# A four-layer network on one core: order of TensorE's work in the state space layers, and quantised stages rebuilt with features on partitions

## The chip, the cores and the metric
The kernel runs on one core of a Trainium2 chip. The metric is the device time of one execution in microseconds, median of the runs. All arithmetic is in float32.

## The reference, cut to what matters
The input x is 8 sequences of 256 tokens with 128 features. Twelve sublayers follow each other; the change touches the second of the middle group (state space layers) and the two quantised feed-forward networks near the end.
```python
for i in range(4):                       # state space layers; x is the normalised input
    xn = layernorm(x, ln_w[i], ln_b[i])
    x_in, z = split(xn @ in_w.T); xc = silu(conv4(x_in) + cb)
    dt_rank, Bm, Cm = split(xc @ xp_w.T); dt = softplus(dt_rank @ dt_w.T + dt_b)
    h_t = h_{t-1} * exp(dt_t * A) + dt_t * xc_t * B_t        # 256 channels x 16 states
    y = sum_n(h_t * C_t) + xc * D
    x = (y * silu(z)) @ out_w.T + x
...
h = x                                     # quantised network; x is the normalised input
for b in range(3):
    y = h @ (dequant(q[2b]) + lb @ la).T + bias[2b]
    y = gelu(layernorm(y, gamma[b], beta[b]))
    h = y @ (dequant(q[2b+1]) + lb @ la).T + bias[2b+1] + h
# used as: x = x + 0.5 * h, before and after the last attention
```

## The kernel before, in words
Each sublayer is a stage of its own with a barrier behind it, at which its semaphores are cleared. x stays on the chip, tokens on partitions. Within a stage every engine has its own instruction stream, in an order written out by hand, and semaphores tie them together. An engine never passes an instruction that waits.

**State space layers** (`state_space_layers`). A unit (l, s) is layer l of sequence s; 32 units follow each other in `over_units`. A unit has NP = 8 slots, one for each pair of states. In slot i: ScalarE makes the decays of slot i + 1 in two PSUM banks (`decays`, L1301, four Exp of 255 columns), VectorE multiplies dt·u by the B rows (`input_term`, L1151; GpSimd does slot 4) and scans (L1173), GpSimd multiplies the state by the C rows one slot later (L1225), TensorE adds these up with the identity as stationary operand two slots later (L1382, four passes a slot) into `y_bank`. In slot 0 of that lag the skip product comes behind it (L1387), in slot 2 the gated result (`yg`, L1158) of the last unit goes through the output product (L1396) together with the old x (L1393), and ScalarE copies it back into `xm` (L1324, slot 4).

The pieces of the next unit (`nxt`) and the one after it (`after`) are prepared in the same slots by `prepare`: slot 0 the xp product, 1 its rows (ScalarE, L1256), 2 the dt product (TensorE, L1349) and Abs and Exp of it (ScalarE, L1259, L1261), 3 two Identities and Ln (L1264 to L1267, Ln and the next Exp each need a table load), 4 the normalised rows of `after` (ScalarE, L1276), 5 their transposes and the gate product of `nxt` (TensorE), 6 the convolution product (L1368), 7 Silu of both (L1286, L1292). On TensorE `prepare(i)` comes last in slot i, behind the sum, the skip product and the output product. All preparation goes through PSUM bank 7.

`stage_state_space` writes the normalised input to `xm`; after the layers a block of its own adds `xm` to x (L1038).

**Quantised stages** (`stage_quantised_ffn`, tags f3a and f3b). Both make the weights `w` anew from the packed integers. The 8 sequences go in two rounds of U = 4. For each of 3 blocks the four sequences pass through one phase after the other: transpose h (L2010), copy, product y with tokens on partitions (L2018), bias added and statistics by VectorE (L1933, L1910, L1913), rstd by GpSimd (L1962, L1965), normalised (L1918), transposed (L2026), Gelu (L1990), second product (L2034), added to h plus bias (L1945, GpSimd L1973).

Of the kernel before, what the change touches and what calls it, by code (L numbers as in the profile page):

```python
# [11 lines left out]
ALU = mybir.AluOpType  # L12
# [3 lines left out]
P = 128  # L16
# [18 lines left out]
    "f3": dict(scale=768, bias=768, la=768, lb=768, gam=3, bet=3),  # L35
# [912 lines left out]
def stage_state_space(K, tag):  # L948
# [3 lines left out]
    with ExitStack() as scope:  # L952
# [92 lines left out]
def state_space_layers(K, tag, m):  # L1045
# [12 lines left out]
    with ExitStack() as scope:  # L1058
# [44 lines left out]
        with nc.Block() as block:  # L1103
# [143 lines left out]
            def _(act):  # L1247
                def prepare(i, nxt, after):
# [62 lines left out]
                def slot(i, now, last, nxt, after):  # L1311
# [23 lines left out]
            def _(pe):  # L1335
# [37 lines left out]
                def slot(i, now, last, nxt, after):  # L1373
                    at = lagged(i, 2, NP, now, last)
# [24 lines left out]
                    prepare(i, nxt, after)  # L1399
# [468 lines left out]
def stage_quantised_ffn(K, tag):  # L1868
    nc = K.nc
    NB, U = 3, 4  # L1870
    with ExitStack() as scope:
        K.scope = scope
        sb = K.sb
        w = sb(f"{tag}_w", [P, 6 * P])
        bn = sb(f"{tag}_bn", [P, U, TS, 6])
        mv = sb(f"{tag}_mv", [P, U, TS, 2])
        rs = sb(f"{tag}_rs", [P, U, TS])
        hcur = sb(f"{tag}_h", [P, U, W])
        hb = sb(f"{tag}_h_bias", [P, U, W])
        ht = sb(f"{tag}_ht", [P, U, W])  # L1880
        y = sb(f"{tag}_y", [P, U, W])
        yn = sb(f"{tag}_yn", [P, U, W])
        gt = sb(f"{tag}_gelu_t", [P, U, W])
        (dve_s, pool_s, lora_ps, w_ready, stats, rstd, h_ready, ht_ps, ht_ready, y_ps, yn_ready, ynt_ps, gt_ready,
         z_ps, hb_ready, pool_hold, y_sb) = make_sems(
            K, tag, "dve_chain pool_chain lora_product w_ready stats rstd h_ready ht_product ht_ready y_product "
                    "yn_ready ynt_product gelu_ready z_product h_bias_ready pool_hold y_ready")
        f = lambda n: field(K, "f3", n)
        bias = f("bias")
        NL = (NB + 1) * U  # L1890
        with nc.Block() as block:
# [3 lines left out]
            def _(dve):  # L1895
                dve.wait_ge(K.loaded["f3"], 16)
                dve.wait_ge(K.loaded_q, 16)
                link = chain(dve, dve_s)

                link(dve.tensor_scalar(w[:, :], K.qw[:, :], 7.5, 1.0 / 7.5, ALU.subtract, ALU.mult))  # L1900
                link(dve.tensor_tensor(w[:, :], w[:, :], f("scale"), ALU.mult))
                dve.wait_ge(lora_ps, 1)
                dve.tensor_tensor(w[:, 0:512], w[:, 0:512], K.ps[0][:, :], ALU.add).then_inc(w_ready, 1)
                dve.tensor_tensor(w[:, 512:768], w[:, 512:768], K.ps[1][:, 0:256], ALU.add).then_inc(w_ready, 1)
                with dve.Fori(0, B // U) as s:
                    link = chain(dve, dve_s)

                    def statistics(u, src):
                        for j in range(TS):
                            i = dve.bn_stats(bn[:, u, j, :], src(j))  # L1910
                        link(i)
                        for j in range(TS):
                            i = dve.bn_aggr(mv[:, u, j, :], bn[:, u, j, :])  # L1913
                        i.then_inc(stats, 1)

                    def normalise(u, src, dst):
                        for j in range(TS):
                            i = dve.tensor_scalar(dst[:, u, j * P:(j + 1) * P], src(j), mv[:, u, j, 0:1],  # L1918
                                                  rs[:, u, j:j + 1], ALU.subtract, ALU.mult)
                        return i  # L1920

                    xt = lambda u: lambda j: K.x[:, bass.ds((s * U + u) * W + j * P, P)]
                    yt = lambda u: lambda j: y[:, u, j * P:(j + 1) * P]
                    for u in range(U):
                        statistics(u, xt(u))
                    for u in range(U):
                        dve.wait_ge(rstd, s * NL + u + 1)
                        normalise(u, xt(u), hcur).then_inc(h_ready, 1)
# [669 lines left out]
```

## Time and profile before

| | |
|---|---|
| median of 3 runs | 3105.43 us (3095.72 to 3110.03) |
| the profiled execution | 3106.51 us |
| its span, first to last instruction | 3104.8 us |
| mean granted TensorE clock | 0.896 of full speed |
| busy: PE, DVE, ACT, POOL | 83%, 65%, 55%, 40% of the span |

"Idle before" is the time in which the engine waited for the instruction named as releaser. Records of matmuls overlap, since the last columns of one drain while the next streams.

### The profile page before, as it was taken

How to read it: one execution, taken by the hardware profiler on the slowest of the kernel's cores; microseconds unless marked ns; L12 is line 12 of the kernel's file. 1: busy time of each engine (PE TensorE's matmuls, PEld its weight loads, DVE VectorE, ACT ScalarE, POOL GpSimd, SP SyncE). 2: the span in 40 equal slices, each digit the busy share in tenths (PEclk: the TensorE clock that was granted, in tenths of full speed). 3: DMA queues.
4: the chain of work that ended last, by engine and by line, in shares of the span. 5: the costliest groups of instructions: out<-in, count | busy, mean ns of one | idle time of the engine just before them, and what ended most of it. 6: DMA issues, size and time to landing. Idle time of an engine off the chain costs nothing. (4 is left out here: it accounts for less than half of the span.)

```text
span 3104.8 us, 39498 instructions
## 1 busy us (share of the span) xinstructions
PE 2575.9 (83%) x11320; PEld 1549.7 (50%) x11320; DVE 2025.0 (65%) x4275; ACT 1696.5 (55%) x3585; POOL 1243.8 (40%) x1144
## 2 busy tenths in 40 slices
PE   7999785688888888888677998688699967988975
PEld 5667532354444444444333443456444444777764
DVE  7888655699999999999644443466344364545445
ACT  4555322788888888888422443577444323555532
POOL 1000102688888888888500000322000052444444
PEclk9999898798989989989898999799899966888866
DMA  2000131333333434333332111000111100000000
GB/s 99 1 1 0 58 83 28 131 142 136 151 140 139 145 136 150 140 136 148 143 82 82 55 60 50 1 1 0 55 55 55 63 15 0 1 0 0 0 1 14
DMA packets 35669, 209.60 MB, mean 68 GB/s; under 512 B 4032, under 2 KB 5184, under 8 KB 14016
## 3 DMA queue, kind: packets, MB, share of 16 engines
q1 hardware_dynamic: 35520, 207.89, 18.8%
q8 instruction: 60, 0.98, 0.1%
q14 instruction: 89, 0.73, 0.1%
HBM read 205.25 MB, written 2.62 MB: 67 GB/s over the span
## 5 line engine op out<-in xcount | busy, mean ns | idle before, releaser
L1382 PE MATMUL banks<-mam_state_c,identity 128*128 128x512 f32 x1024 | 539.7, 662 | 141.8 <-POOL mam_state_c L1225 141.8
L1225 POOL TENSOR_TENSOR mam_state_c<-mam_state,weights_r 128x1024 f32<-128x1024 f32 x256 | 599.9, 2358 | 118.6 <-DVE mam_state L1173 118.5
L1173 DVE TENSOR_TENSOR_SCAN mam_state<-banks,mam_dbu 128x1024 f32<-128x1024 f32 x256 | 580.4, 2278 | 73.1 <-ACT banks L1301 72.5
L1301 ACT ACTIVATE banks<-mam_dt,mam_a_neg 128x255 f32<-128x255 f32 x1024 | 423.3, 461 | 38.3 <-DVE mam_state L1173 36.7
L1382 PEld LDWEIGHTS banks<-mam_state_c,identity 128*128 128x128 f32 x1024 | 200.1, 208 | 399.1 <-issue 199.6
L1151 DVE TENSOR_TENSOR mam_dbu<-banks,weights_r 128x1024 f32<-128x1024 f32 x224 | 267.1, 1204 | 10.4 <-ACT banks L1309 10.4
L2224 POOL TENSOR_TENSOR at_attention<-at_relu 128x512 f32<-128x512 f32 x128 | 130.9, 1040 | 172.9 <-ACT at_relu L2277 88.3
L424 ACT ACTIVATE at_probs<-banks,at_nmax 128x256 f32<-128x256 f32 x256 | 117.7, 472 | 138.4 <-DVE at_nmax L365 134.9
L2402 PEld LDWEIGHTS banks<-at_v,at_attention 128*128 128x128 f32 x1024 | 153.2, 223 | 41.0 <-issue 34.8
L862 DVE TENSOR_TENSOR m2b_hidden<-m2b_gelu,m2b_comb_spread 128x512 f32<-128x512 f32 x128 | 85.9, 690 | 129.2 <-ACT m2b_gelu L889 119.6
L862 DVE TENSOR_TENSOR m2a_hidden<-m2a_gelu,m2a_comb_spread 128x512 f32<-128x512 f32 x128 | 86.0, 690 | 128.9 <-ACT m2a_gelu L889 118.5
L2402 PE MATMUL banks<-at_v,at_attention 128*128 128x64 f32 x1024 | 152.6, 303 | 4.2 <-POOL at_attention L2224 4.2
L889 ACT ACTIVATE m2b_gelu<-banks,weights_r 128x512 f32<-128x512 f32 x128 | 85.2, 685 | 105.2 <-PE banks L909 105.2
L889 ACT ACTIVATE m2a_gelu<-banks,weights_r 128x512 f32<-128x512 f32 x128 | 85.2, 685 | 105.0 <-PE banks L909 104.9
L930 PE MATMUL banks<-m2a_hidden,weights_r 128*128 128x512 f32 x256 | 123.0, 604 | 7.1 <-DVE m2a_hidden L862 7.1
L930 PE MATMUL banks<-m2b_hidden,weights_r 128*128 128x512 f32 x256 | 123.0, 604 | 6.6 <-DVE m2b_hidden L862 6.6
L1706 ACT ACTIVATE at_probs<-at_scores,at_negated_max 128x160 f32<-128x160 f32 x256 | 95.0, 421 | 59.1 <-DVE at_negated_max L1553 58.8
L909 PE MATMUL banks<-m2b_xnt,weights_r 128*128 128x512 f32 x256 | 123.5, 606 | 0.0
L144 POOL TENSOR_SCALAR at_ln_rs<-at_ln_mv 128x2 f32<-128x2 f32 x16 | 4.5, 282 | 294.3 <-DVE at_ln_mv L346 252.9
L909 PE MATMUL banks<-m2a_xnt,weights_r 128*128 128x512 f32 x256 | 122.3, 600 | 0.0
L1368 PE MATMUL banks<-mam_xn_padded,weights_r 128*128 128x256 f32 x512 | 120.8, 390 | 0.7 <-ACT mam_xn_padded L1281 0.7
L1368 PEld LDWEIGHTS banks<-mam_xn_padded,weights_r 128*128 128x128 f32 x512 | 100.4, 196 | 29.0 <-issue 14.3
(483 smaller groups left out, 5304.6 us busy)
## 6 DMA issues: line engine op xcount, KB each, us to landing
weights_r<-mam_bc_rows SPq DMA_DIRECT2D x128, 1024.0 KB, 4.7
m2a_comb_spread<-m2a_comb_rows SPq DMA_DIRECT2D x16, 1024.0 KB, 7.6
m2b_comb_spread<-m2b_comb_rows SPq DMA_DIRECT2D x16, 1024.0 KB, 7.6
m1a_comb_spread<-m1a_comb_rows SPq DMA_DIRECT2D x16, 512.0 KB, 8.1
m1b_comb_spread<-m1b_comb_rows SPq DMA_DIRECT2D x16, 512.0 KB, 8.5
weights_r<-in_mb SPq DMA_DIRECT2D x1, 4332.0 KB, 12.8
weights_r<-in_m SPq DMA_DIRECT2D x1, 4200.0 KB, 13.1
weights_r<-in_a SPq DMA_DIRECT2D x1, 2632.0 KB, 12.1
```

Source lines behind the costliest of these rows:

```text
L862: dve.tensor_tensor(hid[:, g % 3, c, :], gelu[:, g % 2, c, :], comb[:, block_of(p, e // 4) + e % 4, :], ALU.mult).then_inc(hid_ready, 1)
L889: act.activation(gelu[:, g % 2, c, :], h_bank(g, c)[:, :], ACT.Gelu, bias=b1[:, 2 * e + c:2 * e + c + 1]).then_inc(gelu_ready, 1)
L909: pe.matmul(h_bank(g, c)[:, :], w1[:, e * 256 + c * P:e * 256 + (c + 1) * P], R.xnt[:, p % 2, :], start=True, stop=True).then_inc(h_ps, 1)
L930: i = pe.matmul(y[:, :], w2[:, (2 * e + c) * P:(2 * e + c + 1) * P], hid[:, g % 3, c, :], start=False, stop=(e == E - 1 and c == 1))
L1151: dve.tensor_tensor(dbu[:, j % 4, :, :, :], both(K.ps[6][:, :].rearrange("p (c t) -> p c t", c=C)), b_rows(j), ALU.mult).then_inc(dbu_dve, 1)
L1173: dve.tensor_tensor_scan(flat2(h[:, i % 4, :, :, :]), decay(i), flat2(dbu[:, i % 4, :, :, :]), 0.0, ALU.mult, ALU.add).then_inc(h_ready, 1)
L1225: pool.tensor_tensor(hc[:, j % 4, :, :, :], h[:, j % 4, :, :, :], c_rows(j), ALU.mult).then_inc(hc_ready, 1)
L1301: i = act.activation(decay(j)[:, o + 1:o + S], dt[:, q, c, 1:S], ACT.Exp, scale=aneg[:, l, k:k + 1])
L1368: k = pe.matmul(K.ps[7][:, c * S:(c + 1) * S], f(l, "taps")[:, t * 256 + c * P:t * 256 + (c + 1) * P], xpad[:, q, t:t + S], start=(t == 0) ...
L1382: k = pe.matmul(y_bank(q)[:, :], K.ident[:, :], flat(hc[:, j % 4, n, :, :]), start=(j == 0 and n == 0), stop=(j == NP - 1 and n == 1))
L2224: pool.tensor_tensor(at[:, i % 4, :, :], rel[:, i % 4, :, :], rel[:, i % 4, :, :], ALU.mult).then_inc(at_ready, 1)
L2402: k = pe.matmul(K.ps[4 + g % 2][:, t * 256 + r * DV:t * 256 + (r + 1) * DV], at[:, h % 4, j, t * P:(t + 1) * P], v[:, q, j, h * DV:(h + 1) ...
```

## The change
In the state space layers TensorE calls `prepare(i)` first in slot i instead of last. ScalarE issues its two Identities in slot 2, right behind Exp and ahead of the decays that it makes in slot 3 (those of slot 4); Ln stays in slot 3. In the last layer TensorE adds x to the output product with the identity, and ScalarE writes the result to x; the closing addition and its block are gone.

The quantised stages are written anew. Features are on partitions throughout, and the work goes in N = 12 steps m: block m // 4, pair of sequences m % 4 (512 tokens). In slot m TensorE issues the second product z of step m - 4, the spread of rstd over the partitions for step m - 2, the sum of squares over the partitions for step m - 1 and the first product y of step m. The mean over features is taken out of the weights and the bias beforehand, so that only the variance is left to compute: Square on ScalarE, products with a column of ones, a small operation on VectorE, the power on GpSimd, a product of the broadcast column with the identity. The weights are made once, in f3a, and kept. The input is normalised and transposed pair by pair at the start; at the end each pair is transposed back and added to x. The bias comes as six columns in place of 768.
```diff
-    "f3": dict(scale=768, bias=768, la=768, lb=768, gam=3, bet=3),
+    "f3": dict(scale=768, bcol=6, la=768, lb=768, gam=3, bet=3),
...
         state_space_layers(K, tag, dict(locals()))
-        clear_sems(K)
-        add_s, = make_sems(K, tag, "added")
-        with nc.Block() as block:
-            @block.vector
-            def _(dve):
-                dve.tensor_tensor(K.x[:, :], K.x[:, :], xm[:, :], ALU.add).then_inc(add_s, 1)
-                dve.wait_ge(add_s, 1)
 
...
-                    if nxt and i == 3:
                         act.wait_ge(exp_ready, b + 1)
                         act.activation(vu[:, :, :], ve[:, :, :], ACT.Identity, bias=K.ones[:, 0:1]).then_inc(plus_ready, 1)
                         act.wait_ge(plus_ready, b + 1)
                         act.activation(va[:, :, :], vu[:, :, :], ACT.Identity, bias=K.neg_one[:, 0:1]).then_inc(part_ready, 1)
+                    if nxt and i == 3:
                         act.activation(vl[:, :, :], vu[:, :, :], ACT.Ln).then_inc(ln_ready, 1)
                     if after:
                         l, s, q = after
...
-                        act.activation(xm[:, bass.ds(s * W, W)], y_bank(q)[:, 0:W], ACT.Copy).then_inc(done, 1)
+                        res = K.x if l + 1 == L else xm
+                        act.activation(res[:, bass.ds(s * W, W)], y_bank(q)[:, 0:W], ACT.Copy).then_inc(done, 1)
...
                 def slot(i, now, last, nxt, after):
+                    prepare(i, nxt, after)
                     at = lagged(i, 2, NP, now, last)
...
                                       xm[:, bass.ds(s * W + t * P, P)], start=True, stop=False)
+                            if l + 1 == L:
+                                pe.matmul(y_bank(q)[:, t * P:(t + 1) * P], K.ident[:, :],
+                                          K.x[:, bass.ds(s * W + t * P, P)], start=False, stop=False)
                             for c in range(C):
                                 k = pe.matmul(y_bank(q)[:, t * P:(t + 1) * P], yg[:, c, t * P:(t + 1) * P],
                                               f(l, "outw")[:, c * P:(c + 1) * P], start=False, stop=(c == C - 1))
                         k.then_inc(out_ps, 1)
-                    prepare(i, nxt, after)
 
...
+                    firsts = w[:, :].rearrange("p (b a o) -> p b a o", b=NB, a=2)[:, :, 0, :]
+                    link(dve.tensor_reduce(wmean[:, :], firsts, AX_X, ALU.add))
+                    link(dve.tensor_scalar(wmean[:, :], wmean[:, :], 1.0 / P, None, ALU.mult))
+                    dve.tensor_tensor(firsts, firsts, wmean[:, :].unsqueeze(2).broadcast_to([P, NB, P]), ALU.subtract)
...
+                for m in range(N + 5):
+                    n = m - 4
+                    if 0 <= n < N:
+                        dve.wait_ge(z_ps, n + 1)
+                        h = ht[:, n % NP, :]
+                        dve.scalar_tensor_tensor(h, z_bank(n)[:, :], b2(n), h, ALU.add, ALU.add).then_inc(h_ready, 1)
+                    n = m - 2
+                    if 0 <= n < N:
+                        dve.wait_ge(r_ps, n + 1)
+                        dve.wait_ge(y_ready, n + 1)
+                        if n >= 2:
+                            dve.wait_ge(gt_ready, n - 1)
+                        dve.tensor_tensor(yn[:, n % 2, :], yc[:, n % 3, :], r_bank(n)[:, :],
+                                          ALU.mult).then_inc(yn_ready, 1)
+                    n = m - 1
+                    if 0 <= n < N:
+                        dve.wait_ge(var_ps, n + 1)
+                        if n >= 2:
+                            dve.wait_ge(ys_ready, n - 1)
+                        dve.tensor_scalar(var[:, n % 2, :], v_cols(n), 1.0 / P, EPS, ALU.mult,
+                                          ALU.add).then_inc(var_ready, 1)
+                    if m + 2 < NP:
+                        norm_sums(m + 2)
+                        norm_apply_pair(m + 2)
+                    p = m - 5 - (NB - 1) * NP
+                    if 0 <= p < NP:
+                        dve.wait_ge(o_ps, p + 1)
+                        x = K.x[:, p * WP:(p + 1) * WP]
+                        dve.scalar_tensor_tensor(x, y_bank(m)[:, :], 0.5, x, ALU.mult, ALU.add).then_inc(added, 1)
 
...
+                for n in range(N):
+                    if n + 2 < NP:
+                        norm_root(n + 2)
+                    pool.wait_ge(var_ready, n + 1)
+                    if n >= 2:
+                        pool.wait_ge(r_ps, n - 1)
+                    pool.tensor_tensor(ys[:, n % 2, :], var[:, n % 2, :], K.neg_half[:, 0:TP],
+                                       ALU.pow).then_inc(ys_ready, 1)
...
+                for m in range(N + 2):
+                    n = m - 2
+                    if 0 <= n < N:
+                        act.wait_ge(yn_ready, n + 1)
+                        if n >= 2:
+                            act.wait_ge(z_ps, n - 1)
+                        act.activation(gt[:, n % 2, :], yn[:, n % 2, :], ACT.Gelu, bias=f("bet")[:, n // NP:n // NP + 1],
+                                       scale=f("gam")[:, n // NP:n // NP + 1]).then_inc(gt_ready, 1)
+                    if m < N:
+                        act.wait_ge(y_ps, m + 1)
+                        if m >= 2:
+                            act.wait_ge(var_ps, m - 1)
+                        act.activation(sq[:, m % 2, :], y_bank(m)[:, :], ACT.Square, bias=b1(m)).then_inc(sq_ready, 1)
+                        if m >= 3:
+                            act.wait_ge(yn_ready, m - 2)
+                        act.activation(yc[:, m % 3, :], y_bank(m)[:, :], ACT.Identity, bias=b1(m)).then_inc(y_ready, 1)
+                    if m + 1 < NP:
+                        transposed_input(m + 1)
 
             @block.tensor
...
+                for m in range(N + 5):
+                    n = m - 4
+                    if 0 <= n < N:
+                        pe.wait_ge(gt_ready, n + 1)
+                        if n < 2:
+                            pe.wait_ge(ht_ready, n + 3)
+                        else:
+                            pe.wait_ge(h_ready, n - 1)
+                        c = 2 * (n // NP) + 1
+                        pe.matmul(z_bank(n)[:, :], w[:, c * P:(c + 1) * P], gt[:, n % 2, :],
+                                  start=True, stop=True).then_inc(z_ps, 1)
+                    n = m - 2
+                    if 0 <= n < N:
+                        pe.wait_ge(ys_ready, n + 1)
+                        if n < 2:
+                            pe.wait_ge(ht_ready, n + 1)
+                        else:
+                            pe.wait_ge(yn_ready, n - 1)
+                        for j in range(TP):
+                            k = pe.matmul(r_bank(n)[:, j * P:(j + 1) * P], ys[:, n % 2, j:j + 1].broadcast_to([P, P]),
+                                          K.ident[:, :], start=True, stop=True)
+                        k.then_inc(r_ps, 1)
+                    n = m - 1
+                    if 0 <= n < N:
+                        pe.wait_ge(sq_ready, n + 1)
+                        if n >= 1:
+                            pe.wait_ge(var_ready, n)
+                        for j in range(TP):
+                            k = pe.matmul(v_cols(n)[:, j:j + 1], sq[:, n % 2, j * P:(j + 1) * P], K.ones[:, 0:1],
+                                          start=True, stop=True)
+                        k.then_inc(var_ps, 1)
+                    if m < N:
+                        p = m % NP
+                        if m >= 3:
+                            pe.wait_ge(y_ready, m - 2)
+                        if m < NP:
+                            pe.wait_ge(ht_ready, m + 1)
+                        else:
+                            pe.wait_ge(h_ready, m - NP + 1)
+                        c = 2 * (m // NP)
+                        pe.matmul(y_bank(m)[:, :], w[:, c * P:(c + 1) * P], ht[:, p, :],
+                                  start=True, stop=True).then_inc(y_ps, 1)
+                        if m + 1 < NP:
+                            transposed_input(m + 1)
+                    p = m - 5 - (NB - 1) * NP
+                    if 0 <= p < NP:
+                        pe.wait_ge(h_ready, (NB - 1) * NP + p + 1)
+                        pe.wait_ge(y_ready, min(N, m - 2))
+                        if p >= 3:
+                            pe.wait_ge(added, p - 2)
+                        for j in range(TP):
+                            k = pe.transpose(y_bank(m)[:, j * P:(j + 1) * P], ht[:, p, j * P:(j + 1) * P], K.ident[:, :])
+                        k.then_inc(o_ps, 1)
...
```

## Rows read from the trace of the kernel before

**Rows 1.** The page, busy times and the granted clock in 40 slices of 77.6 us.
```profile
...
PE 2575.9 (83%) x11320; PEld 1549.7 (50%) x11320; DVE 2025.0 (65%) x4275; ACT 1696.5 (55%) x3585; POOL 1243.8 (40%) x1144
...
PEclk9999898798989989989898999799899966888866
...
```

**Rows 2.** Windows by stage: length, busy PE, PEld, DVE, ACT, POOL, clock, DMA.
```profile
...
1200.00:1400.00 200.00, 171.33 (x516) 93.17 (x515) 182.51 (x142) 166.15 (x334) 174.35 (x109) 0.91 0.39 142
2480.00:2584.00 104.00, 63.72 (x300) 51.32 (x300) 63.89 (x252) 21.38 (x48) 50.88 (x112) 0.70 0.05 18
...
```

**Rows 3.** Waits of DVE, ACT, PE in 620 to 1460 us: total, times, longest.
```profile
...
DVE mam_state L1173 <- ACT banks L1301: 65.2, 43, 1.9
...
ACT mam_dt_abs L1259 <- PE banks L1349: 80.8, 28, 3.0
...
ACT mam_conv L1286 <- PE banks L1368: 18.2, 14, 1.4
...
PE banks L1382 <- POOL mam_state_c L1225: 114.5, 59, 3.5
...
```

**Rows 4.** Groups of instructions, 620 to 1460 us: busy, mean ns, idle before.
```profile
...
L1173 DVE TENSOR_TENSOR_SCAN mam_state<-banks,mam_dbu 128x1024 f32<-128x1024 f32 x226 | 512.6, 2278 | 65.4 <-ACT banks L1301 65.2
...
L1301 ACT ACT_TABLE_LOAD x56 | 71.8, 1283 | 1.0
...
L1142 DVE SCALAR_TENSOR_TENSOR mam_dt_correction<-banks,mam_dt_correction 128x512 f32<-128x512 f32 x28 | 19.2, 686 | 2.4 <-POOL mam_dt_correction L1189 0.2
...
```

**Rows 5.** Timeline of parts of two units: start, duration, instruction, idle before.
```profile
...
1006.76 3.78 PE L1382 MATMUL banks<-mam_state_c,identity 128*128 128x512 f32 x4 [3.31 <-POOL mam_state_c L1225]
...
1012.47 2.12 PE L1382 MATMUL banks<-mam_state_c,identity 128*128 128x512 f32 x4
...
1022.39 3.70 PE L1382 MATMUL banks<-mam_state_c,identity 128*128 128x512 f32 x8
...
1028.22 1.13 PE L1349 MATMUL banks<-mam_bc_dt_rows,weights_r 9*128 9x256 f32 x4
...
1029.39 0.60 ACT L1259 ACTIVATE mam_dt_abs<-banks 128x512 f32<-128x512 f32 x1 [2.88 <-PE banks L1349]
...
1038.66 2.29 DVE L1173 TENSOR_TENSOR_SCAN mam_state<-banks,mam_dbu 128x1024 f32<-128x1024 f32 x1 [1.86 <-ACT banks L1301]
1038.73 0.87 ACT L1276 ACTIVATE mam_ln_xn<-mam_xm,mam_ln_bias,mam_ln_rs 128x128 f32<-128x128 f32 x2
...
```

**Rows 6.** Timeline at the end of the state space layers.
```profile
...
1526.82 0.38 ACT L1324 ACTIVATE mam_xm<-banks 128x256 f32<-128x256 f32 x1 [10.89 <-PE banks L1396]
1530.20 2.29 DVE L1038 TENSOR_TENSOR x<-x,mam_xm 128x2048 f32<-128x2048 f32 x1 [5.08 <-PEq L67]
...
1533.36 0.87 DVE L604 BATCH_NORM_STATS2 m1b_ln_bn<-x 128x6 f32<-128x128 f32 x4 [0.86 <-PEq L67]
...
```

**Rows 7.** Timeline, first and last work of both quantised stages.
```profile
...
2480.64 2.87 PE L1998 MATMUL banks<-weights_r 32*128 32x128 f32 x12 [2.92 <-PEq L67]
...
2580.85 1.35 DVE L1950 SCALAR_TENSOR_TENSOR x<-f3a_h,x 128x256 f32 x3
...
2997.36 2.90 PE L1998 MATMUL banks<-weights_r 32*128 32x128 f32 x12 [4.00 <-PEq L67]
...
3096.01 1.79 DVE L1950 SCALAR_TENSOR_TENSOR x<-f3b_h,x 128x256 f32 x4
...
```

**Rows 8.** Durations of like operations, from timelines and a group.
```profile
...
1535.06 1.02 POOL L547 TENSOR_TENSOR m1b_ln_rs<-m1b_ln_rs,neg_half 128x4 f32<-128x4 f32 x1
...
1538.50 0.60 ACT L652 ACTIVATE m1b_xnt<-banks 128x512 f32<-128x512 f32 x1 [11.30 <-PE banks L556]
...
1539.15 1.89 PE L563 MATMUL banks<-weights_r,m1b_xnt 128*128 128x16 f32 x8 [0.69 <-ACT m1b_xnt L652]
...
L889 ACT ACTIVATE m2a_gelu<-banks,weights_r 128x512 f32<-128x512 f32 x128 | 85.2, 685 | 105.0 <-PE banks L909 104.9
...
2505.50 1.06 PE L2018 MATMUL banks<-f3a_w,f3a_ht 128*128 128x128 f32 x8
...
```

More of the change, by code:

```diff
@@ L1888, in stage_quantised_ffn @@
-        f = lambda n: field(K, "f3", n)
-        bias = f("bias")
-        NL = (NB + 1) * U
+        w = K.f3_w
+        wmean = sb(f"{tag}_w_mean", [P, NB])
+        bcol = K.f3_b
+        bn = sb(f"{tag}_bn", [P, NP, TP, 6])
+        mv = sb(f"{tag}_mv", [P, NP, TP, 2])
+        rs = sb(f"{tag}_rs", [P, NP, TP])
+        xn = sb(f"{tag}_xn", [P, 2, WP])
+        ht = sb(f"{tag}_ht", [P, NP, WP])
+        yc = sb(f"{tag}_y", [P, 3, WP])
+        sq = sb(f"{tag}_y_squares", [P, 2, WP])
+        var = sb(f"{tag}_y_var", [P, 2, TP])
@@ L1891, in stage_quantised_ffn @@
+        f = lambda n: field(K, "f3", n)
+        first = tag == "f3a"
+        y_bank = lambda m: K.ps[m % 3]
+        r_bank = lambda m: K.ps[3 + m % 2]
+        z_bank = lambda m: K.ps[5 + m % 2]
+        t_bank = lambda p: (r_bank, z_bank)[p // 2](p)
+        b1 = lambda m: bcol[:, 2 * (m // NP):2 * (m // NP) + 1]
+        b2 = lambda m: bcol[:, 2 * (m // NP) + 1:2 * (m // NP) + 2]
+        v_cols = lambda m: K.ps[7][:, (m % 2) * 8:(m % 2) * 8 + TP]
         with nc.Block() as block:
@@ new lines, in norm_root @@
+                def norm_root(p):
+                    pool.wait_ge(stats, p + 1)
+                    pool.tensor_scalar(rs[:, p, :], mv[:, p, :, 1], EPS, None, ALU.add).then_inc(eps_in, 1)
+                    pool.wait_ge(eps_in, p + 1)
+                    pool.tensor_tensor(rs[:, p, :], rs[:, p, :], K.neg_half[:, 0:TP], ALU.pow).then_inc(rstd, 1)
+                norm_root(0)
+                norm_root(1)
+                for n in range(N):
[6 more added lines that the diff above has]
+                                       ALU.pow).then_inc(ys_ready, 1)
@@ L1979, in _, with transposed_input @@
             @block.scalar
             def _(act):
-                act.wait_ge(K.loaded["f3"], 16)
-                with act.Fori(0, B // U) as s:
-                    for b in range(NB):
-                        e = s * (NB * U) + b * U
-                        for u in range(U):
-                            act.wait_ge(ht_ps, e + u + 1)
-                            act.activation(ht[:, u, :], K.ps[0 + u % 2][:, 0:W], ACT.Copy).then_inc(ht_ready, 1)
-                        for u in range(U):
-                            act.wait_ge(ynt_ps, e + u + 1)
-                            act.activation(gt[:, u, :], K.ps[4 + u % 2][:, 0:W], ACT.Gelu, bias=f("bet")[:, b:b + 1],
-                                           scale=f("gam")[:, b:b + 1]).then_inc(gt_ready, 1)
+                def transposed_input(p):
+                    act.wait_ge(xt_ps, p + 1)
+                    act.activation(ht[:, p, :], t_bank(p)[:, :], ACT.Copy).then_inc(ht_ready, 1)
@@ new lines, in _, with transposed_input @@
+                if first:
+                    for i in range(6):
+                        k = pe.matmul(K.ps[i // 4][:, (i % 4) * P:(i % 4 + 1) * P], f("la")[0:32, i * P:(i + 1) * P],
+                                      f("lb")[0:32, i * P:(i + 1) * P], start=True, stop=True)
+                    k.then_inc(lora_ps, 1)
+                    pe.matmul(K.ps[2][:, 0:6], K.ones[:, :], f("bcol"), start=True, stop=True).then_inc(bias_ps, 1)
+                def transposed_input(p):
+                    pe.wait_ge(xn_ready, p + 1)
+                    for j in range(TP):
+                        k = pe.transpose(t_bank(p)[:, j * P:(j + 1) * P], xn[:, p % 2, j * P:(j + 1) * P], K.ident[:, :])
+                    k.then_inc(xt_ps, 1)
@@ L2566, in host_arrays @@
     g["f3"] = dict(scale=np.repeat(i["L3_ffn_scales"].transpose(2, 0, 1), 16, axis=0).reshape(P, -1),
-                   bias=rows(i["L3_ffn_biases"]), la=pad(i["L3_ffn_lora_a"].transpose(1, 0, 2).reshape(32, -1)),
+                   bcol=i["L3_ffn_biases"].T, la=pad(i["L3_ffn_lora_a"].transpose(1, 0, 2).reshape(32, -1)),
                    lb=pad(i["L3_ffn_lora_b"].transpose(2, 0, 1).reshape(32, -1)),
```

182 lines of the change are left out of this document (54 added, 128 removed).

## The prediction, blind

> **What bounds the kernel now.** I read the page first: PE is busy 83% of the span, DVE 65%, and the granted clock is lowest, 0.6 to 0.8 of full, in slices 33 and 34 and in the last two [rows 1]. Those are the two quantised stages. The windows by stage then say what kind of stage each is. In the state space layers DVE is busy 182.5 of 200 us, POOL 174, PE 171, ACT 166: four nearly full engines. In a quantised stage nothing is full: PE and DVE 64 of 104 us, ACT 21, at a clock of 0.70 [rows 2]. The first is short of one engine's time, the second is a chain in which engines take turns.
>
> State space layers. A unit is one sequence of one layer, 32 in all, of 8 slots. The 226 scans in 840 us are 28.25 units, so a unit takes 29.7 us. DVE waits 65.2 us there, all for ACT's decays: 2.3 us a unit, so DVE's own floor is 29.7 - 2.3 = 27.4 us. ACT in turn waits 80.8 us, 28 times, in front of Abs for the dt product of PE (2.9 us a unit), and 18.2 us for the convolution product. PE waits for POOL 114.5 us, 4.05 a unit [rows 3, 4]. The timeline shows why the dt product is late. PE works without a break from the sum at 1006.76: through the sums of slots 5, 6, 7, 0 and 1 with the preparation between them, at 1022.39 the last sum of one unit and the first of the next (eight passes), then the skip product and the output product, and only at 1028.22 the dt product. ACT had stood 2.88 us when it got it, at 1029.39. Ln, two table loads and decays 5 follow on ACT, and the scan of slot 5 starts 1.86 us late, at 1038.66 [rows 5]. The reader should see that the order on PE, not its load, makes this wait: the sum, skip and output product in front are wanted by nobody yet.
>
> Quantised stages: from 2480.64 to 2582.2 (101.6 us) and from 2997.36 to 3097.8 (100.4 us) [rows 7].
>
> **Part 1, preparation ahead of the sums.** Nothing is removed, only order changes: dt is now issued before the slot's sum, skip and output product. From the last sum's end (1022.39 + 1.85 = 1024.2) to the dt product was 4.0 us and becomes nothing. ACT's two Identities (0.7 us each) move ahead of decays 4, where ACT has about 4 us in hand while scan 3 runs: no cost. No DMA is moved. What is queued behind the new position: in slot 5 the sum stands behind the transposes, which wait for ACT's normalised rows; in slots 0 and 6 sums stand behind the xp and convolution products. In return the convolution product comes one sum (1.7 us) earlier, which covers ACT's 18.2 us.
>
> What is late next? There are two loops. DVE's is its own work, 27.4 us. The other goes through PE: dt product, ACT to the end of its normalised rows (from 1028.22 to 1039.6 = 11.4 us, in which ACT does not idle after Abs), then PE from there to the last sum. That PE work is the same set as before, 1006.76 to 1024.2 = 17.4 us. Sum: 28.8 us, more than 27.4. But 17.4 contains a stretch at half clock: the four passes at 1006.76 take 3.78 us where eight take 3.70 at 1022.39, after an idle of 3.31 us [rows 5]. The half clock lasts until about the passes at 1012.47, which take 2.12 us for four again: 5.7 us, which cost half of that, 2.9 us, more than at full clock. Without it the loop is 25.9 us and DVE rules. The new idle ahead of slot 5, from sum 2's end to the normalised rows, I work out as 2.5 to 3.1 us, too near to 3.31 to say. So a unit is 27.4 to 28.8 us. I take the middle, 28.1: 1.6 us a unit, x 32 = 51 us. Bounds: 74 us (2.3 x 32) above; below, 28.8 us and 0.3 us more at each of the two places where sums now queue, 10 us. I keep 0 as a rival.
>
> **Part 2, last layer in place.** PE gets two products of 128 columns a unit in 8 units (0.4 us each, in PE's slack). DVE's addition goes with its block: after the last ACT instruction (1527.2) the long clearing stays, the addition (2.29 us) and the 0.86 us behind it go [rows 6]. Gain 3 us, bounds 2 and 5.
>
> **Part 3, quantised stages.** Work is now in steps of one pair of sequences and one block: 12 steps a stage, features on partitions, so that both transposes within a block vanish. For each step:
> PE: two products of 512 columns, each two passes. Eight such passes take 3.70 us with the last one's drain, a pitch of about 0.43 [rows 5], so 0.86 a product and 1.72 for two. The spread of rstd is four products of 128 columns, eight passes, 1.06 us by L2018 alone, 0.86 when others follow and its drain is covered [rows 8]. The variance is four products with one moving column but full 128-column loads: the nearest row is L563, eight passes of 16 columns in 1.89 us at half clock, so about 0.9 at full. Sum 3.5 us.
> ACT: Gelu, Square, Identity of 512 columns, 0.685 each by L889 [rows 8], 2.1 us. DVE: two operations of 512 columns at 0.69 by L1142 [rows 4] and a small one, 1.5 us. POOL: a power on 4 columns, 1.02 us [rows 8].
> PE is the longest. Does it run without gaps? In a slot of the new order z, the rstd spread and the variance are issued before y, and cover Square (y to variance of the next slot) and DVE's h (0.7 us, under 1.8 us of PE work). Variance, DVE, power (0.15 + 1.02) lies under y and z of 1.7 us. So in the middle PE sets the pace, at 3.5 us, and a busy PE keeps its clock; I take 3.6.
>
> The variance is where a page and a row part. The Trainium skill, "TensorE: Matmul & The Clock Gate", section "Wait — 56ns, not 53.3ns?", says that starts never come closer than about 25 ns however few the columns; by that alone, an estimate, the eight passes would take 0.2 us, a step 2.8 us and both stages 17 us less. No run here shows it; L563, which loads 128 columns per pass as this does, stands against it.
>
> Start of a stage: norm of a pair from 1533.36 to the end of the copy at 1539.1 is 5.7 us in a stage of the same form [rows 6, 8]. Then the first four steps can't fill PE: they wait for norms of pairs 2 to 4, which DVE does between them (a pair is 3.9 us from first statistic to normalised rows, two of which stand in front of the first variance), and at half clock. About 4 us a step: 16 us. Eight steps at 3.6: 29. Tail of the last pair: Square, variance, power, spread, multiply, Gelu, product, add, transpose, add: 0.7+0.9+0.2+1.0+0.9+0.7+0.7+0.9+0.7+0.5+0.7 = 7.9, with handovers 8. Together 5.7 + 16 + 29 + 8 = 58.7 us; 58 for f3b. f3a also makes its weights (conversion, scaling, two adds, mean and its removal, bias), partly beside the norm: 3 us more, 61. f3b loses that wholly. Gain 101.6 - 61 + 100.4 - 58 = 83 us. Bounds from both sides: a stage without start-up loss is 5.7 + 42 + 8 = 56, minus the variance's whole 0.9 x 12 that is 45 (gain 109 with f3a's 3 us); one with 5 us in all steps is 74 (gain 51).
>
> **Sum.** Profiled execution 3106.5 us (span 3104.8), 1.1 us above the median of 3105.4. 51 + 3 + 83 = 137. 3105.4 - 137 = 2968, I say 2969.
>
> **Rivals.** All in us of the median; likeliest case above, 0.50, own range 2945 to 2995.
> Clock kept, DVE rules the unit (27.4) and a quantised step is nearer 3.2: 74 + 3 + 93, 2935. For it: the new gap may stay under 3.31 us. Against: a gap of nearly that size stands in the same place. 0.18.
> The state space wait only changes its name: DVE's gating waits for the last sum, now behind one more product, and a unit stays 29.7. Gain 86, 3019. For it: PE is unbroken from 1006.76 to the dt product. Against: the reordered pieces are not on the loop. 0.12.
> Quantised steps bound by handovers or by table loads around Square (two of 1.28 us a step [rows 4] make ACT 4.6 us against 3.5): 1.1 x 12 x 2 = 26 less, 2995; at 5 us in the eight middle steps, 22 less and the first four longer too, 3000. Nothing in the trace shows a load ahead of a Square, and none shows Gelu with Square. 0.15.
> Slower: the half-clock stretch grows. In a unit it is now 5.7 us and costs 2.9. A unit must exceed 29.7 + 86/32 = 32.4 to undo parts 2 and 3; the loop is 25.9 + half the stretch, so the stretch must exceed 13 us. Then every further 2 us cost 32: at 18 us a unit is 34.9, 3186. The Trainium skill has this in "TensorE: Matmul & The Clock Gate", section "HAM oscillation": a PE that idles each round starts each round at half clock. Here the clock in the stage is 0.91, so it recovers each time. 0.03.
> The same clock in the quantised stages alone (steps of 7 us) takes the 83 away: 3051, still faster. 0.02.
>
> **Range and chances.** The first four cases cover 2935 to 3019, so 2930 to 3020 leaves out less than 0.2. A measurement of this kernel can't tell 0.5% (15 us) from nothing. All cases but the slower one are beyond it: faster 0.96, same 0.01, slower 0.03.
>
> **What the profile should show.** ACT's wait before Abs gone or under 0.5 us a unit; DVE's wait for decays under 1 us, perhaps a new DVE wait for the last sum before the gating; unit 28.1 us. Quantised stages of about 61 and 58 us, PE over 85% busy in their middle with the clock near full, variance passes near 0.11 us each, one table load at most. The prediction fails if the unit keeps its length, or if steps take over 4.5 us.

## The result and the profile after

The changed kernel takes 2966.8 us (2959.5 to 2970.5, 4 runs) against 3105.4 us; the ratio is 0.9555 (0.9525 to 0.9584). Forecast was 2969. The profiled execution has a span of 2963.2 us, 141.6 less than before.

The page first, against [rows 1]: slices 33 and 34, at a granted clock of 0.6 before, are at 0.8 now.
```profile
...
PE 2525.2 (85%) x11310; PEld 1514.2 (51%) x11310; DVE 1957.2 (66%) x3955; ACT 1711.4 (58%) x3566; POOL 1177.3 (40%) x960
...
PEclk9999989699999999999989999799989988899868
...
```
Windows of the same two kinds of stage, against [rows 2] (columns as there). The state space layers have DVE at 196 of 200 us instead of 182.5 (over the whole of 620 to 1400 us it is 757 of 780, at a clock of 0.94). The middle of a quantised stage has PE busy without a break, at full clock.
```profile
...
1200.00:1400.00 200.00, 175.43 (x579) 97.24 (x578) 195.95 (x152) 180.72 (x356) 185.52 (x118) 0.97 0.40 151
2446.00:2474.00 28.00, 28.00 (x162) 20.31 (x161) 12.76 (x25) 16.59 (x25) 8.05 (x8) 1.00 0.01 1
...
```
Waits in the state space layers, 620 to 1400 us, against [rows 3]: total, times, longest.
```profile
...
DVE mam_y_gated L1151 <- PE banks L1377: 17.7, 21, 1.4
DVE mam_state L1166 <- ACT banks L1294: 3.4, 8, 0.6
...
ACT mam_dt_abs L1252 <- PE banks L1343: 4.4, 6, 0.8
...
PE banks L152 <- ACT mam_ln_xn L1269: 84.5, 27, 3.3
...
```
In these 780 us there are 222 scans, 27.75 units. ACT's wait before Abs fell from 2.9 to 0.16 us a unit, DVE's wait for decays from 2.3 to 0.1. A new wait has come, the one the prediction named: DVE's gating waits 0.64 us a unit for the last sum. PE now idles 3.0 us a unit before the transposes. The timeline, against [rows 5]:
```profile
...
996.75 1.13 PE L1343 MATMUL banks<-mam_bc_dt_rows,weights_r 9*128 9x256 f32 x4
...
1007.70 0.86 ACT L1269 ACTIVATE mam_ln_xn<-mam_xm,mam_ln_bias,mam_ln_rs 128x128 f32<-128x128 f32 x2
...
1008.71 0.66 PE L152 MATMUL banks<-identity,mam_ln_xn 128*128 128x128 f32 x2 [3.26 <-ACT mam_ln_xn L1269]
...
1009.16 1.92 PE L1354 MATMUL banks<-mam_xn_padded,weights_r 128*128 128x256 f32 x4
...
1021.06 3.70 PE L1377 MATMUL banks<-mam_state_c,identity 128*128 128x512 f32 x8
...
1024.69 1.13 PE L1343 MATMUL banks<-mam_bc_dt_rows,weights_r 9*128 9x256 f32 x4
1024.80 0.69 DVE L1151 TENSOR_TENSOR mam_y_gated<-banks,mam_gate 128x512 f32<-128x512 f32 x1 [0.62 <-PE banks L1377]
...
1025.86 0.60 ACT L1252 ACTIVATE mam_dt_abs<-banks 128x512 f32<-128x512 f32 x1
...
```
The transposes come after an idle of 3.26 us, and the gate product behind them runs at half clock (1.92 us for four passes of 256 columns, 1.03 at full clock). The last sum of the unit (second half of the row at 1021.06; it ends at 1024.76, and the gating starts at 1024.80) is followed at once by the dt product, 1.2 us before Abs.

From the first scan to the end of the last there are 950.8 us before and 895.8 after: a unit is 29.71 and 27.99 us. This measure is used for all runs below. It comes from one profiled execution of each kernel; e7, which leaves the layers of the changed kernel as they are, gave 28.12, so differences of 0.1 us say nothing.

End of the layers, against [rows 6]: 3.0 us from the last ACT instruction to the next stage, where 6.2 us stood.
```profile
...
1471.78 0.38 ACT L1318 ACTIVATE x<-banks 128x256 f32<-128x256 f32 x1 [11.33 <-PE banks L1394]
...
1475.16 0.87 DVE L604 BATCH_NORM_STATS2 m1b_ln_bn<-x 128x6 f32<-128x128 f32 x4 [5.53 <-PEq L67]
...
```
Both quantised stages, against [rows 7]: f3a from 2419.40 to 2482.8, 63.4 us; f3b from 2897.30 to 2957.0, 59.7 us.
```profile
...
2419.40 0.87 DVE L1912 BATCH_NORM_STATS2 f3a_bn<-x 128x6 f32<-128x128 f32 x4 [2.05 <-PEq L67]
...
2426.75 2.07 PE L2089 MATMUL banks<-f3a_ht,f_weights 128*128 128x512 f32 x2 [1.33 <-DVE f_bias L1947]
...
2444.57 1.02 PE L2058 MATMUL banks<-f3a_gelu_t,f_weights 128*128 128x512 f32 x2
...
2462.09 1.02 PE L2058 MATMUL banks<-f3a_gelu_t,f_weights 128*128 128x512 f32 x2
...
2462.95 1.05 PE L2068 MATMUL banks<-identity,f3a_y_rs 128*128 128x128 f32 x8
...
2463.84 0.95 PE L2077 MATMUL banks<-ones,f3a_y_squares 128*128 128x1 f32 x8
...
2464.65 1.10 PE L2089 MATMUL banks<-f3a_ht,f_weights 128*128 128x512 f32 x2
...
2465.59 1.02 PE L2058 MATMUL banks<-f3a_gelu_t,f_weights 128*128 128x512 f32 x2
...
2482.09 0.69 DVE L1981 SCALAR_TENSOR_TENSOR x<-banks,x 128x512 f32<-128x512 f32 x1
...
```
```profile
...
2897.30 0.87 DVE L1912 BATCH_NORM_STATS2 f3b_bn<-x 128x6 f32<-128x128 f32 x4 [3.44 <-PEq L67]
...
2903.09 2.07 PE L2089 MATMUL banks<-f3b_ht,f_weights 128*128 128x512 f32 x2 [0.69 <-ACT f3b_ht L2006]
...
2917.70 1.92 PE L2058 MATMUL banks<-f3b_gelu_t,f_weights 128*128 128x512 f32 x2
...
2956.32 0.69 DVE L1981 SCALAR_TENSOR_TENSOR x<-banks,x 128x512 f32<-128x512 f32 x1 [0.15 <-PE banks L2100]
...
```
The five rows from 2462.09 are one step: z, spread, variance, y, and the next z 3.50 us later. Their starts are 0.81 to 0.94 us apart, with no idle noted.

### The profile page after: what moved, and what is told of

Its sections match the earlier page's. It is cut to its first block and busy times, and to the rows that moved or that the text cites. A ratio compares the mean times of both kernels' runs of the same rounds, so it can differ in the third digit from the quotient of the medians.

```text
span 2963.2 us, 38455 instructions
## 1 busy us (share of the span) xinstructions
PE 2525.2 (85%) x11310; PEld 1514.2 (51%) x11310; DVE 1957.2 (66%) x3955; ACT 1711.4 (58%) x3566; POOL 1177.3 (40%) x960
## 3 DMA queue, kind: packets, MB, share of 16 engines
q8 instruction: 62, 1.02, 0.1%
## 5 line engine op out<-in xcount | busy, mean ns | idle before, releaser
L1377 PE MATMUL banks<-mam_state_c,identity 128*128 128x512 f32 x1024 | 507.0, 633 | 9.9 <-POOL mam_state_c L1218 9.4
L152 PE MATMUL banks<-identity,mam_ln_xn 128*128 128x128 f32 x64 | 17.4, 363 | 127.6 <-ACT mam_ln_xn L1269 127.6
```

Of the source, the lines that this page charges most:

```text
L1377: k = pe.matmul(y_bank(q)[:, :], K.ident[:, :], flat(hc[:, j % 4, n, :, :]), start=(j == 0 and n == 0), stop=(j == NP - 1 and n == 1))
```

## The experiments

Every kernel is the one before or the changed one with one edit. A total also moves with stages that no edit touches: the last attention stage took 412.5 us in the changed kernel's profile, 402.9 in e4's and 398.6 in e12's, at granted clocks of 0.82, 0.84 and 0.86. So a unit's length is the better witness for the state space layers.

| run | unit, us | total, us | ratio to before |
|---|---|---|---|
| before | 29.71 | 3102 to 3105 | 1 |
| e1, TensorE's order alone | 30.26 | 3124.2 | 1.0063 (1.0041 to 1.0085) |
| e9, ScalarE's Identities alone | 29.52 | 3099.5 | 0.9981 (0.9967 to 0.9994) |
| e3, both | 28.24 | 3054.2 | 0.9845 (0.9818 to 0.9872) |
| e2, dt product alone | 28.72 | 3070.4 | 0.9897 (0.9874 to 0.992) |
| e11, before, gap filled | 29.16 | 3087.0 | 0.994 (0.9923 to 0.9957) |
| changed | 27.99 | 2966.8 | 0.9555 (0.9525 to 0.9584) |
| e4, changed, TensorE's order undone | 29.61 | 3004.2 | 0.9679 (0.9642 to 0.9717) |
| e5, changed, gap filled | 27.47 | 2939.7 | 0.9483 (0.9463 to 0.9504) |
| e10, two fillers | 27.56 | 2946.4 | 0.9493 (0.9477 to 0.9509) |
| e6, rows early | 28.79 | 2987.7 | 0.964 (0.9621 to 0.966) |
| e8, more work on TensorE | 28.72 | 2983.0 | 0.9613 (0.9587 to 0.9639) |
| e7, one variance product | 28.12 | 2955.9 | 0.9527 (0.9504 to 0.955) |
| e12, starts filled | 27.49 | 2946.9 | 0.9499 (0.9484 to 0.9515) |

**e1, TensorE's order alone.**
```diff
 def slot(i, now, last, nxt, after):       # TensorE
+    prepare(i, nxt, after)
     at = lagged(i, 2, NP, now, last)
...
-    prepare(i, nxt, after)
```

> The kernel before, with one edit: TensorE prepares first in each slot of the state space layers; ScalarE's order stays. My theory (the dt product came late because of the order on TensorE): the wait before Abs falls from 2.9 us a unit to under 0.5, a unit takes 28.1 to 28.3 us instead of 29.7, the total 3105 - 50 = 3055 us. Rival (the wait only changes its name, or ScalarE's move is what gives the gain): a unit stays above 29.2 us, the total 3090 or more.

It is 0.6% slower than before, and my theory fell as I had put it. The waits (620 to 1400 us, 25.5 units):
```profile
...
DVE mam_state L1173 <- ACT banks L1301: 42.5, 36, 1.7
DVE mam_y_gated L1158 <- PE banks L1383: 35.9, 26, 1.4
...
ACT banks L1301 <- DVE mam_state L1173: 65.3, 75, 1.7
...
```
The timeline shows the chain. ACT makes Abs and Exp early, then waits 1.74 us for a scan before decays 4, and only behind them come the Identities, the normalised rows, and PE's transposes after an idle of 4.68 us:
```profile
...
1000.35 1.12 PE L1349 MATMUL banks<-mam_bc_dt_rows,weights_r 9*128 9x256 f32 x4
...
1004.51 1.66 ACT L1301 ACTIVATE banks<-mam_dt,mam_a_neg 128x255 f32<-128x255 f32 x4 [1.74 <-DVE mam_state L1173]
...
1006.12 0.71 ACT L1264 ACTIVATE mam_dt_one_plus<-mam_dt_exp,ones 128x512 f32<-128x512 f32 x1
...
1012.71 0.87 ACT L1276 ACTIVATE mam_ln_xn<-mam_xm,mam_ln_bias,mam_ln_rs 128x128 f32<-128x128 f32 x2
...
1013.72 0.66 PE L152 MATMUL banks<-identity,mam_ln_xn 128*128 128x128 f32 x2 [4.68 <-ACT mam_ln_xn L1276]
...
```
From the dt product to the end of the rows it is 13.2 us, not 11.4. PE's work from the transposes to the end of the last sum takes 17.4 us as before, and the next dt product starts 30.7 us after this one. So DVE waits for the last sum (1.4 us a unit) and still for decays (1.7).

**e2, only the dt product first.** Edit: `if i == 2: prepare(...)` ahead of the sum, all other slots behind it.

> The kernel before, with only the preparation of slot 2 (the dt product) ahead of its sum, all other slots as before. If the dt product carries the gain: a unit of 28.3 us, the total about 3062 us; the wait of 0.65 us a unit before the convolution's Silu stays. Rival (the convolution product, the transposes and xp being earlier carry it): 29.2 us a unit or more, 3090.

A unit of 28.72 us, between the 28.3 of the theory and the 29.2 of the rival: this one move gives 1.0 us, with the Identities unmoved. The sum of slot 5 isn't held up by the transposes here. What stays is what the later pieces would bring:
```profile
...
DVE mam_state L1173 <- ACT banks L1301: 25.1, 31, 1.4
...
ACT mam_xn_padded L1281 <- PE banks L152: 32.3, 23, 2.2
ACT mam_conv L1286 <- PE banks L1368: 22.7, 22, 1.6
...
```
**e3, order and Identities, and e9, Identities alone.**
```diff
-                    if nxt and i == 3:
                         act.wait_ge(exp_ready, b + 1)
                         act.activation(vu[:, :, :], ve[:, :, :], ACT.Identity, ...)
                         act.wait_ge(plus_ready, b + 1)
                         act.activation(va[:, :, :], vu[:, :, :], ACT.Identity, ...)
+                    if nxt and i == 3:
                         act.activation(vl[:, :, :], vu[:, :, :], ACT.Ln)
```

> The kernel before with the whole of part 1, TensorE's order and ScalarE's two Identities. Theory: the Identities are hidden, so this is within 5 us of the run with TensorE's order alone, near 3053 us. Rival: the Identities cost, or give, 10 us or more.

> The kernel before with ScalarE's two Identities in slot 2 alone. TensorE's order alone was slower than before (3124 us), both were 3054, and undoing TensorE's order in the changed kernel gave 3004 where 3024 was forecast. Theory now: the Identities fill the time in which ScalarE would wait for a scan, so moving them is worth about 20 us with the old order of TensorE and 70 with the new: 3083 us here, a unit of 29.1 us. Rival (the 20 us came with the quantised stages or the last layer in place): 3103 us.

The total of e3 is the one expected, but the reason was wrong: it is 2.0 us a unit shorter than e1, not equal. e9 is 0.2 us a unit shorter than before. So the Identities are worth 0.2 us with the old order and 2.0 with the new. With the new order ACT has Exp done while a scan runs; put there, the Identities fill the wait. With the old order Abs came so late (74.0 us of waiting in 780 in e9) that there was no such wait to fill. The forecast for e9, 3083 us and a unit of 29.1, was missed: the 20 us that it sought to explain in e4 are not the Identities'.

**e4, TensorE's order undone in the changed kernel.** The reverse of e1's edit.

> The changed kernel with TensorE preparing last again. Theory: parts add up, so the unit returns to 29.7 us and the total is 3105 - 79 (quantised stages by the trace after) - 3 = 3023 us. Rival (the parts overlap, or the last layer in place already helped the state space layers): under 3010 us.

3004 us, 19 less than expected. The unit is 29.61, as forecast. The two profiled executions say where the rest lies. e4's is 98.1 us shorter than that of the kernel before: 3 from the first scan to the last, 3 at the end of the last layer, 82 in the quantised stages (61.6 and 58.0 us here) and 10 in the untouched attention stage between them (405.0 us from the end of f3a to the start of f3b, against 415.2). So the parts add up in the layers, and the rival's overlap is not what made the total short; why the attention stage was shorter stays open.

**e5, the gap filled, and e10, filled less.** Five (e10: two) products with a zero stationary operand, added behind slot 4's sum; the result doesn't change.
```diff
+                        if j == 2:
+                            for n in range(5):
+                                pe.matmul(y_bank(q)[:, 0:S], zero[:, :], skip[:, 0, :, :].rearrange("p c t -> p (c t)"),
+                                          start=False, stop=False)
```

> The changed kernel; in slot 4 TensorE adds, behind the sum, five products of a zero stationary operand with 256 constant columns (ten passes, 2.1 us), so that it idles 1.2 us instead of 3.3 before the transposes. Result unchanged. Theory (the half-clock stretch behind that gap is what keeps a unit at 28.1 us above VectorE's 27.4): the granted clock in the layers goes from 0.94 to near 1.00, VectorE's wait for the last sum goes, a unit takes 27.5 us, the total 2967 - 19 = 2948 us. Rival (order and handovers set it, not the clock): 2967 us or more, for TensorE has more to do.

> The changed kernel with two zero products of 256 columns (0.85 us) behind slot 4's sum instead of five. Theory (the clock falls because of the idle, and a shorter idle of about 2.4 us keeps most of it): granted clock 0.98 or more in the layers, 2945 us. Rival (only an idle near 1 us keeps it, as five products left): clock near 0.94, 2960 us or more.

Waits and window of e5:
```profile
...
PE banks L152 <- ACT mam_ln_xn L1271: 20.3, 28, 0.7
...
```
```profile
...
620.00:1400.00 780.00, 726.18 (x2501) 418.60 (x2500) 773.69 (x593) 709.52 (x1412) 734.96 (x452) 1.00 0.42 154
...
```
The idle before the transposes is 0.7 us at most, the clock 1.00 where it was 0.94, the wait for the last sum is gone, and a unit takes 27.47 us, within 0.1 of the 27.4 us that the prediction gave DVE's own work. With more work on PE the kernel is 27 us shorter. Of these the layers give 17 (0.52 us a unit); the rest stands in stages that the edit doesn't touch. Two fillers do nearly the same: PE waits up to 2.4 us, the clock in the layers is 0.99, a unit 27.56. The advice in the Trainium skill, "TensorE: Matmul & The Clock Gate", section "HAM oscillation", to leave TensorE no long idle in each round, is borne out here: an idle of 3.3 us each unit goes with half clock behind it, one of 2.4 us mostly doesn't.

**e11, the gap filled in the kernel before.** The same edit.

> The kernel before with five zero products (2.1 us) behind slot 4's sum, nothing else. Theory (17.4 us of TensorE's work, of which 2.9 us are owed to half clock, stand in front of the dt product): the dt product comes about 2 to 3 us earlier, ScalarE's wait before Abs shrinks from 2.9 to under 1 us and a unit from 29.7 to about 28.4: 3062 us. Rival (clock is not what holds the old order): 3095 us or more.

The clock is 1.00 here too, but a unit is 29.16 us and ACT still waits 73.4 us before Abs. 3087 us lies between the theory (3062) and the rival (3095 or more), nearer the rival: full clock alone gives 0.55 us a unit of the 2.3 that DVE waits. PE, now ahead, stands in front of the first sum of the unit until GpSimd has its product, with the dt product behind it:
```profile
...
1017.75 1.96 PE L1384 MATMUL banks<-mam_state_c,identity 128*128 128x512 f32 x4 [1.02 <-POOL mam_state_c L1227]
...
1021.84 1.13 PE L1351 MATMUL banks<-mam_bc_dt_rows,weights_r 9*128 9x256 f32 x4
...
```
So before the change it was in the main the order, with or without the clock.

**e6, the normalised rows ahead of the decays of slot 5.** ScalarE's block for slot 4 is called before `decays`.

> The changed kernel; in slot 4 ScalarE makes the normalised rows ahead of the decays instead of behind them. Theory (loop from the last sum through ScalarE to the transposes): rows come 1.7 us earlier, TensorE's gap shrinks below 2 us, decays 5 come 0.8 us later with about 1 us in hand: a unit of 27.6 us, 2950 us. Rival (the decays have nothing in hand): VectorE waits for them, 2970 us or more.

Slower by 0.8 us a unit. The rows come early, but the transposes write bank 7, which the dt product holds until DVE's correction (L1135) has read it:
```profile
...
DVE mam_state L1166 <- ACT banks L1298: 13.7, 39, 0.7
...
PE banks L152 <- DVE mam_dt_correction L1135: 59.0, 26, 2.5
PE banks L1364 <- ACT mam_xm L1323: 27.3, 23, 1.6
...
DVE mam_y_gated L1151 <- PE banks L1387: 27.8, 27, 1.4
...
```
The wait went from the rows to the bank (26 times, up to 2.5 us), and the gate product (L1364) now waits for ScalarE's copy as well. Together PE idles 86 us there, where it idled 84.5 for the rows in the changed kernel. DVE waits 0.5 us a unit for decays and 1.0 for the last sum, 1.5 in place of 0.8. What stood ready was not what was needed last.

**e8, more work on TensorE.** Four of the same products (1.7 us) behind the sum of slot 6.

> The changed kernel with four more products of 256 columns with a zero stationary operand (1.7 us) behind the sum of slot 6. Theory (the loop through TensorE closes at about 28 us, so its work counts): a unit goes from 28.1 to between 29.0 and 29.8 us, the total 2967 + 29 to 54, about 3010 us, and VectorE waits for the last sum. Rival (VectorE's own work sets the unit, TensorE has 12% in hand): 28.3 us, at most 2975 us.

The unit is 0.73 us longer, DVE's wait for the last sum 1.6 us (42.2 us in 27 units): between theory (29.0 to 29.8 us) and rival (28.3). Of 1.7 us of added work 1.0 is hidden. Part of that is probably the clock, which the fillers lift from 0.94 to 0.96.

**e7, one variance product of four.**
```diff
-                        for j in range(TP):
-                            k = pe.matmul(v_cols(n)[:, j:j + 1], sq[...], K.ones[:, 0:1], ...)
+                        for j in range(1):
+                            k = pe.matmul(v_cols(n)[:, 0:TP], sq[...], K.ones[:, 0:TP], ...)
```

> The changed kernel with one of the four variance products in each step of the quantised stages; three of four tiles get the first one's sum of squares, so the result differs. Theory (TensorE's own work sets the step): a step shortens from 3.50 by 3 x 2 passes x 0.107 = 0.64 us to 2.86, both stages together by 0.64 x 12 x 2 = 15, the total 2952 us. Rival (handovers or ScalarE set the step): 3.4 us or more, 2965 us.

The step falls from 3.50 to 3.10 us, less than the 0.64 us of work taken out: it lies between theory (2.86) and rival (3.4 or more). From the variance to y it is now 0.15 us instead of 0.81, but the spread starts 1.02 us after z and not 0.86, and the variance 0.99 after the spread and not 0.89:
```profile
...
2457.61 1.01 POOL L1999 TENSOR_TENSOR f3a_y_rs<-f3a_y_var,neg_half 128x4 f32<-128x4 f32 x1 [2.09 <-DVE f3a_y_var L1972]
2457.65 1.02 PE L2058 MATMUL banks<-f3a_gelu_t,f_weights 128*128 128x512 f32 x2
...
2458.67 0.97 PEld L2068 LDWEIGHTS banks<-identity,f3a_y_rs 128*128 128x128 f32 x8 [0.82 <-POOL f3a_y_rs L1999]
2458.67 1.16 PE L2068 MATMUL banks<-identity,f3a_y_rs 128*128 128x128 f32 x8
...
2459.66 0.28 PE L2077 MATMUL banks<-ones,f3a_y_squares 128*128 128x4 f32 x2
2459.81 1.10 PE L2089 MATMUL banks<-f3a_ht,f_weights 128*128 128x512 f32 x2
2459.86 0.69 DVE L1965 TENSOR_TENSOR f3a_yn<-f3a_y,banks 128x512 f32<-128x512 f32 x1 [0.40 <-PE banks L2068]
...
2460.47 0.16 DVE L1972 TENSOR_SCALAR f3a_y_var<-banks 128x4 f32<-128x4 f32 x1
...
```
PE's work sets the step at 3.50. At 3.10 another loop does, and the rows show it closed: the spread at 2458.67 lets DVE's multiply go at 2459.86, the small operation on the variance stands behind the multiply at 2460.47, GpSimd's power follows it and takes 1.01 us, and the weight load of the next spread, 3.09 us after the last, waits for that power (0.82 us of idle). In the changed kernel the same power ends 0.38 us before the spread starts (2458.06 + 1.01 against 2459.45). DVE's small operation ahead of its multiply would shorten this loop; that was not tried.

**e12, the starts of the quantised stages filled.** On top of e5, unused products ahead of what PE waits for.

> The changed kernel with the five zero products in slot 4, and TensorE kept busy with unused products of 128 columns in the first microseconds of both quantised stages (12, 6 and 4 of them ahead of what it would wait for). Theory (the first four steps run at a clock of 0.57 in the first of the stages): they gain 2 to 3 us each, 2935 us against 2940 without. Rival (the starts wait for VectorE's norms, not TensorE): 2940 us or a little more.

No gain in the median (2946.9 against 2939.7, intervals overlap). The clock does rise (0.84 in the first 21 us of f3a, 1.00 behind), but the first four steps wait for DVE's norms one after the other. f3a takes 61.6 us with and without the unused products, f3b 59.7 us with them and 58.0 without. The rival holds.

## Why the prediction was right

Its terms against the trace, gains in us: state space layers 51, measured 55.0 (950.8 - 895.8). Last layer in place 3, measured 3.2. Quantised stages 83, measured 38.2 + 40.7 = 78.9. Sum 137 and 137; the spans differ by 141.6, the rest lies in untouched stages. That the sums agree to 1 us is luck: the layers gave 4 more than forecast and the quantised stages 4 less, and the attention stage alone moves by 10 us between kernels that share it (e4).

**Part 1.** DVE's floor of 27.4 us is right (27.47 in e5). The loop through PE, its half-clock stretch after the idle before slot 5 and the new wait of the gating are as described: 11.8 us from the dt product at 996.75 to the end of the rows at 1008.56, then 16.1 us from the transposes to the end of the last sum in this unit and 17.4 in the next, where the half clock lasts through the sum behind the gate product (3.62 us for four passes). The next two dt products start 27.9 and 29.3 us after the one before each, and the mean unit is 27.99. e5 shows that the clock makes the difference between 28.0 and 27.5. That the unit came out near 28.1 says less: 28.1 was the middle between two cases, not worked out. One step failed, though it didn't spoil the sum: "ACT's two Identities move ahead of decays 4 ...: no cost". They are not a bystander. I took the 11.4 us from dt product to rows out of a trace in which Abs came so late that ACT did not wait for a scan between Abs and the rows. With TensorE's order alone it is 13.2 us and a unit takes 30.3 us (e1), longer than before. That it is 11.8 us and not 13.2 in the changed kernel is owed to the Identities, which move as well. And "the order on PE, not its load, makes this wait" is confirmed by e11, where PE at full clock changes little.

**Part 3.** Steady step 3.6, measured 3.50, set by PE at full clock. The variance was sized by L563, and that held: eight passes of one column take 0.81 us from their start to that of y, and taking six of them out in e7 gave 0.66, 0.11 a pass. The floor of 25 ns that the Trainium skill gives in "TensorE: Matmul & The Clock Gate", section "Wait — 56ns, not 53.3ns?", is no price for a float32 pass with its own load. Start: 7.4 us in f3a (8.7 forecast) and 5.8 in f3b (5.7). First four steps: 17.8 and 14.6, forecast 16. In other runs of the same code they are shorter: e5's first z of f3a starts 23.4 us into the stage, not 25.2; two of its y products run at half clock (2.07 us) and not three. Its stages take 61.6 and 58.0 us in place of 63.4 and 59.7. Tail from the eighth full step on: 10.2 in both, forecast 8, the mis-sized term: z, h, transposition and addition of four pairs pass one behind another on PE and DVE.

**Rivals.** The unit at 27.4 didn't come, but two fillers nearly bring it (27.56 in e10). No table load stands at Square; f3b has one load, ahead of its first Gelu. The slower case (a longer half-clock stretch) didn't come; the danger on that side lay in leaving out half of part 1.

## What to carry to other kernels

When an instruction is moved forward, redo the waits of what follows on the other engines as they will be then: an interval read from the old trace holds no waits that the old lateness hid. Two edits can be worth nothing or less one by one and 1.5 us a round together. If an engine that owes much to its clock idles a few microseconds in each round, some harmless work in the idle can be worth more than the next reordering (here 0.5 us a unit, 17 us over the layers, where e6's reordering lost 0.8 a unit).

## What the hardware showed beyond that

GpSimd's power on 4 columns took 1.72 us once in f3a's start and 1.01 to 1.04 us in the other 31 of the two stages; the small operation before it took 0.44 against 0.22. Beside the slow ones VectorE converted and scaled the 768-column weights:
```profile
...
2421.16 0.96 DVE L1934 TENSOR_TENSOR f_weights<-f_weights,weights_r 128x768 f32<-128x768 f32 x1
2421.30 1.72 POOL L1989 TENSOR_TENSOR f3a_rs<-f3a_rs,neg_half 128x4 f32<-128x4 f32 x1
...
```
It is one place; whether the one slows the other was not tried. And Gelu from SBUF on 512 columns took 0.81 us here, where Gelu from PSUM in the expert stages took 0.685 [rows 8]. The two differ in the scale too, a column of values here and none there, so no run shows that the source is the cause. ScalarE had time for it.
